# A mixture-of-experts layer on one core: in the experts' second matrix, high rows times high and low weights as one 512-column product in a bank of its own per row tile

## The chip, the cores and the metric

The kernel runs on one core of a Trainium2 chip. Time is device time in microseconds (us), from a run of the whole program. TensorE (PE) multiplies, ScalarE (ACT), VectorE (DVE) and GpSimd (POOL) work on rows and columns, SyncE (SP) issues most transfers. A core has eight PSUM banks of 512 float32 columns.

## What is computed

Three stages over 4096 rows of 256 columns: x + 0.5 FFN(norm x), then x + attention(norm x), then x + 0.5 FFN(norm x). The change touches the experts of both FFN stages:

```python
topk_w, topk_idx = jax.lax.top_k(scores, cap)       # 16 experts, 256 rows of each of 2 batches
x_tok = jnp.take_along_axis(hidden_states[:, None, :, :], topk_idx[..., None], axis=2)
g = jnp.einsum('becd,efd->becf', x_tok, Wg)
u = jnp.einsum('becd,efd->becf', x_tok, Wu)
h = jax.nn.gelu(g, approximate=False) * u           # 512 hidden columns
eo = jnp.einsum('becf,edf->becd', h, Wd) * topk_w[..., None]
flat = flat.at[flat_idx].add(eo.reshape(-1, d))
out = flat + shared                                 # the shared expert
```

## The kernel before

Each FFN stage goes through 24 items of 512 rows: items 0 to 7 are the shared expert on all rows, items 8 to 23 the 16 experts (J = 8, NI = 24). In the first FFN stage (`lead`) the last three items are mixed from two experts each. A float32 product is made of three on rounded parts: high x high, high x low, low x high (`product3`, lines 349 to 353). So columns, weights and hidden values each exist as a high part, made by ScalarE (a copy that rounds), and a low part, made by VectorE (the difference).

The engines work in steps s, each in an order written out by hand. In step s of the expert stretch:

- TensorE makes gate and up of item s - 1 in four pieces f, gu(s, 0) and gu(s, 1), then down of item d = s - 2 (`down`, line 905), then gu(s, 2) and gu(s, 3). A piece is 12 products of 512 columns into one bank of pG and one of pU. down is four row tiles q of 12 products of 256 columns, two tiles to a bank (pD). Before it writes a piece's pG bank, gelu of two pieces before must be done, and before the pU bank mul of two pieces before.
- ScalarE (lines 1156 to 1186): gelu(s, f) of each piece, high(s, f) of the hidden values, split(s, w) for the high part of the three weights of item s, join_planes(s) (two copies at L1069 and one at L1072), which joins the turned halves of item s's gathered columns (turned_planes, which the profile calls outing_turned_planes in the first and uting_turned_planes in the second stage), and part_planes(s + 1) (L1062), which parts the next item's rows into 16-bit planes.
- VectorE (lines 1518 to 1535): mul(s, f) = gelu x up into hf, low(s, f), split (low parts, L756), evacuate(s, 0), lower(s) (low part of the joined columns, L1308), evacuate(s, 1), gate_weights(s), split(s, 2), mul(s, 2) and so on. evacuate scales a half of down by the gate weight and 0.5 into the SBUF tile eo (L1333).
- SyncE: per expert load_weight for the three weights, each when VectorE has split the one before from the same buffer, and behind raw_d's load turn_planes (L773), a transposing transfer of the planes that part_planes made. Its landing releases join_planes one step on.
- POOL: four scatters of item s - 2's rows (L1571) after the evacuations, then four gathers of a later item's rows (L1547).

The last steps of the first FFN stage (s = 21 to 23) have an order of splits of their own on both engines (`last_steps`, line 1393, and lines 1166 to 1180).

## Time and profile before

| | |
|---|---|
| median of 3 runs | 1497.14 us (1496.7 to 1497.23) |
| profiled execution: its time | 1497.23 us |
| profiled execution: its span | 1495.5 us |
| busy in the span: PE | 1459.6 us (98%) |
| ACT | 1084.9 us (73%) |
| DVE | 891.5 us (60%) |
| POOL | 568.4 us (38%) |

The first FFN stage takes up the first third of the span, attention the middle, the second FFN stage the last third from some 1060 us on. Expert items run from about 190 to 455 and from about 1225 to 1490 us. A share over the whole span mixes these stages; what a change in the experts is worth is read from a step of theirs.

### The profile page before, as it was taken

To read this page: it belongs to the slowest core of one execution; us is meant where nothing else is said; L and a number is where in the kernel's file an instruction comes from. 1 tells how busy PE (TensorE), PEld (TensorE's weight loads), DVE (VectorE), ACT (ScalarE), POOL (GpSimd) and SP (SyncE) were. 2 spreads that over 40 slices of the span, in tenths; PEclk is the share of its full clock that TensorE was granted. 3 is DMA by queue.
4 is the path that set the end of the run, shared out by engine and by line. 5 is a ranking of instruction groups with operands and counts; after the bars stand their busy time and mean duration, and the time that the engine had idled before them with its cause. 6 is when DMAs were issued, how large, how long until landed. Compare 5 with 4: busy or idle time off the path is not lost. (4 is left out here: it accounts for less than half of the span.)

```text
span 1495.5 us, 26581 instructions
## 1 busy us (share of the span) xinstructions
PE 1459.6 (98%) x9857; PEld 1020.4 (68%) x9861; DVE 891.5 (60%) x1984; ACT 1084.9 (73%) x1391; POOL 568.4 (38%) x500
## 2 busy tenths in 40 slices
PE   5999999999999999999999999999999999999998
PEld 4788888888897763333343343333688888888887
DVE  7888777677657971222145152126788867776774
ACT  7322277777746889999999999999622247777772
POOL 5000357776546961112111121111300045666645
PEclk9999999999999999999999999999999999999999
DMA  9212287898846798505337162212511158878873
GB/s 306 78 57 71 87 222 181 187 201 198 192 71 187 248 282 181 87 1 87 51 83 136 33 130 45 43 61 68 159 50 67 57 162 176 214 181 194 194 164 43
DMA packets 180402, 195.74 MB, mean 131 GB/s; under 512 B 77296, under 2 KB 142320, under 8 KB 177520
## 3 DMA queue, kind: packets, MB, share of 16 engines
q1 hardware_dynamic: 152096, 146.30, 38.9%
q0 software_dynamic: 28176, 47.73, 15.1%
q8 instruction: 79, 1.29, 0.4%
q14 instruction: 51, 0.42, 0.1%
HBM read 123.73 MB, written 55.57 MB: 120 GB/s over the span
## 5 line engine op out<-in xcount | busy, mean ns | idle before, releaser
L2507 ACT ACTIVATE 6351_pr<-6351_pS 128x1024 f32<-128x1024 f32 x448 | 420.6, 1196 | 3.1 <-PE 6351_pS L2399 3.1
L2430 PE MATMUL 6351_pO<-6351_pr,6336_vres 128*32 128x512 f32 x1792 | 238.2, 605 | 0.0
L2399 PEld LDWEIGHTS 6351_pS<-sq_rows,sk_rows 50*128 50x128 f32 x896 | 77.7, 184 | 180.2 <-ACT 6351_pr L2507 133.6
L2399 PE MATMUL 6351_pS<-sq_rows,sk_rows 50*128 50x512 f32 x896 | 184.2, 469 | 2.3 <-issue 1.3
L2531 POOL TENSOR_SCALAR_AFFINE_SELECT 6351_pr<-6351_pr 128x512 f32<-128x512 f32 x32 | 20.5, 642 | 358.7 <-ACT 6351_pr L2507 358.7
L351 PE MATMUL 6362_pGU<-columns_ahead,weights_wts 128*128 128x512 f32 (+1 forms) x400 | 155.5, 389 | 0.2 <-DVE 6362_hf L1297 0.2
L352 PE MATMUL 6362_pGU<-columns_ahead,weights_wts 128*128 128x512 f32 (+1 forms) x400 | 152.6, 381 | 0.0
L353 PE MATMUL 6362_pGU<-columns_ahead,weights_wts 128*128 128x512 f32 (+1 forms) x400 | 152.4, 381 | 0.0
L351 PE MATMUL 93_pGU<-columns_ahead,weights_wts 128*128 128x512 f32 (+1 forms) x368 | 143.1, 389 | 1.7 <-issue 1.3
L1106 ACT ACTIVATE hidden_hT<-93_hf 128x512 fp32r<-128x512 f32 x96 | 60.6, 632 | 112.5 <-DVE 93_hf L1297 112.3
L352 PE MATMUL 93_pGU<-columns_ahead,weights_wts 128*128 128x512 f32 (+1 forms) x368 | 140.1, 381 | 0.0
L353 PE MATMUL 93_pGU<-columns_ahead,weights_wts 128*128 128x512 f32 (+1 forms) x368 | 139.9, 380 | 0.0
L1106 ACT ACTIVATE hidden_hT<-6362_hf 128x512 fp32r<-128x512 f32 (+1 forms) x100 | 61.4, 614 | 105.8 <-DVE 6362_hf L1297 105.8
L1571 POOL DMA_INDIRECT out<-eo,6362_idx x64 | 104.7, 1636 | 81.9 <-issue 44.9
L1571 POOL DMA_INDIRECT x_after_ffn<-eo,93_idx x60 | 101.9, 1699 | 77.0 <-DVE eo L1333 48.9
L2584 DVE TENSOR_TENSOR rows_acc<-6351_pO,rows_acc 128x512 f32<-128x512 f32 x30 | 20.8, 692 | 172.6 <-PE 6351_pO L353 172.5
L2541 DVE STREAM_TRANSPOSE 6351_tO<-6351_pO 128x512 f32<-128x512 f32 (+1 forms) x33 | 23.0, 699 | 156.4 <-PE 6351_pO L2430 155.3
L351 PE MATMUL 6362_pD<-weights_wts,hidden_hT 128*128 128x256 f32 x376 | 107.6, 286 | 0.0
L352 PE MATMUL 6362_pD<-weights_wts,hidden_hT 128*128 128x256 f32 x376 | 106.4, 283 | 0.0
L353 PE MATMUL 6362_pD<-weights_wts,hidden_hT 128*128 128x256 f32 x376 | 106.3, 283 | 0.0
L351 PE MATMUL 93_pD<-weights_wts,hidden_hT 128*128 128x256 f32 x352 | 100.8, 286 | 0.0
L352 PE MATMUL 93_pD<-weights_wts,hidden_hT 128*128 128x256 f32 x352 | 99.6, 283 | 0.0
(437 smaller groups left out, 3581.8 us busy)
## 6 DMA issues: line engine op xcount, KB each, us to landing
93_raw_g<-WgT SPq DMA_DIRECT2D x16, 512.0 KB
93_raw_u<-WuT SPq DMA_DIRECT2D x16, 512.0 KB, 3.9
93_raw_d<-WdT SPq DMA_DIRECT2D x16, 512.0 KB, 5.0
q_rows<-rows_halves SPq DMA_DIRECT2D x8, 1024.0 KB, 5.5
k_rows<-rows_halves SPq DMA_DIRECT2D x8, 1024.0 KB, 5.1
6362_raw_g<-WgT SPq DMA_DIRECT2D x16, 512.0 KB
6362_raw_u<-WuT SPq DMA_DIRECT2D x16, 512.0 KB, 3.7
6362_raw_d<-WdT SPq DMA_DIRECT2D x16, 512.0 KB, 4.6
```

The source lines that it names most:

```text
L351: pe.matmul(out, w_hi, x_hi, start=start, stop=False)
L352: pe.matmul(out, w_hi, x_lo, start=False, stop=False)
L353: return pe.matmul(out, w_lo, x_hi, start=False, stop=stop)
L1106: s_hh.done(a.activation(hT[0][:, i % 2, f, cut], hf[:, f % 2, cut], ACT.Copy))
L1571: sent = g.indirect_dma_start(out, bass.IndirectOffsetOnAxis(place_of(item, q), 0), eo[:, k, q, :], None, compute_op=ALU.add)
L2399: m = t_.matmul(to[:, e, :], key, query, start=True, stop=True)
L2430: m = t_.matmul(pO[e * 32:(e + 1) * 32, j % 2, off:off + wd], vres[:, (g // GB) * TPB + kt, at:at + 32], from_(e), start=n == first[j], st ...
L2507: s_exp.done(a.activation(to, pS[:, u % RING, :, :], ACT.Exp, scale=HD ** -0.5))
L2531: s_mask.done(g.affine_select(out=blk_, in_=blk_, compare_op=ALU.is_ge, fill=0.0, base=0, pattern=[[0, GH], [1, P]], channel_multiplier=-1))
L2541: s_copy.done(v.transpose(tO[:, part], pO[:, j % 2, part]))
L2584: s_free.done(v.tensor_tensor(two, from_.rearrange("p (t d) -> p t d", d=D), two, ALU.add))
```

## The change

For items 8 to 21 of either stage (`wide`), the high hidden rows are multiplied with the high and the low down weights side by side, as one product of 512 columns, into a bank of its own for each row tile: the two banks of pD, pX and pC (`wide_bank`). The low rows times the high weights stay a product of 256 columns, added to the first half of the bank. So the sum of a row tile stands in two halves. ScalarE takes the second half, scaled by the gate weight, into eo (`half_out`, L1102 of the changed kernel); VectorE adds the first half to it, scaled alike (L1374). The down weights lie so that high and low stand side by side for each chunk of rows. The factor 0.5 goes into the gate weights. The order of the splits at the end of the first stage comes from one function (`split_in`), and VectorE runs steps 21 to 23 in the common loop.

```diff
             def weight(k, w, h):
+                if w == 2:
+                    return down_pair(k)[:, :, h * D:(h + 1) * D]
                 return wts[k][:, 2 * w + h, :].rearrange("p (c f) -> p c f", c=FC if w == 2 else DC)
+
+            def down_pair(k):
+                return wts[k][:, 4:6, :].rearrange("p h f -> p (h f)").rearrange("p (c w) -> p c w", c=FC)
+
+            wide = lambda d: J <= d < NI - 2
+            wide_bank = lambda q: (pL(0), pX[:, :], pL(1), pC[:, :])[q]
...
+            def split_in(s, at):
+                if lead and s == NI - 3 and at >= 3:
+                    return [(s + 1, at - 3)]
+                if lead and s == NI - 2:
+                    return [(s, 2)] if at == 0 else [(s + 1, at - 1)] if at < 3 else []
+                if lead and s == NI - 1:
+                    return [(s, 2)] if at == 0 else []
+                return [(s, at)] if at < 3 else []
...
+                    if wide(d):
+                        last = c == FC - 1
+                        if c == 0:
+                            t_.matmul(to, hT[0][:, d % 2, c, rows_], down_pair(k)[:, c, :], start=True, stop=False)
+                        m = t_.matmul(to[:, 0:D], hT[1][:, d % 2, c, rows_], weight(k, 2, 0)[:, c, :], start=False, stop=False)
+                        if c > 0:
+                            m = t_.matmul(to, hT[0][:, d % 2, c, rows_], down_pair(k)[:, c, :], start=False, stop=last)
+                        return m
...
-                            m = rows_down(d, q, c, pD[:, q // 2, q % 2, :])
+                            m = rows_down(d, q, c, wide_bank(q) if wide(d) else pD[:, q // 2, q % 2, :])
...
+                def half_out(s, h):
+                    d = s - 2
+                    k = d % 2
+                    if not wide(d):
+                        return
+                    if h == 0:
+                        s_so[k].wait(a, J // 2)
+                        s_sc[k].wait(a, (d - J) // 2)
+                        s_wt.wait(a, d - J + 1)
+                    a.wait_ge(*s_D.at(2 * d + h + 1))
+                    for q in (2 * h, 2 * h + 1):
+                        m = a.activation(eo[:, k, q, :], wide_bank(q)[:, D:2 * D], ACT.Copy, scale=wt[:, k, q:q + 1])
+                    s_half.done(m)
...
-                        own_weights = s < NI - (2 if lead else 0)
                         gelu(s, 0)
-                        if own_weights:
-                            split(s, 0)
+                        splits(s, 0)
                         high(s, 0)
                         gelu(s, 1)
-                        if own_weights:
-                            split(s, 1)
+                        splits(s, 1)
                         high(s, 1)
-                        if lead and s == NI - 2:
-                            split(s, 2)
-                            split(s + 1, 0)
                         if s == BY_PE:
                             gathered(s)
                         else:
                             join_planes(s)
-                        if own_weights:
-                            split(s, 2)
+                        half_out(s, 0)
+                        splits(s, 2)
+                        half_out(s, 1)
+                        gelu(s, 2)
                         if lead and s == NI - 3:
-                            split(s + 1, 0)
-                            split(s + 1, 1)
-                        if lead and s == NI - 2:
-                            split(s + 1, 1)
-                            split(s + 1, 2)
-                        gelu(s, 2)
-                        if s < NI - 1:
+                            splits(s, 3)
+                        elif s < NI - 1:
                             part_planes(s + 1)
                         high(s, 2)
-                        hidden(s, 3)
+                        gelu(s, 3)
+                        splits(s, 4)
+                        if lead and s == NI - 3:
+                            part_planes(s + 1)
+                        high(s, 3)
                         continue
...
-                    v.wait_ge(*s_D.at(2 * d + h + 1))
+                    if wide(d):
+                        v.wait_ge(*s_half.at(2 * (d - J) + h + 1))
+                    else:
+                        v.wait_ge(*s_D.at(2 * d + h + 1))
                     for r in range(2):
                         q = 2 * h + r
-                        if d < J:
+                        if wide(d):
+                            m = v.scalar_tensor_tensor(eo[:, k, q, :], wide_bank(q)[:, 0:D], wt[:, k, q:q + 1], eo[:, k, q, :],
+                                                       ALU.mult, ALU.add)
+                        elif d < J:
                             m = v.scalar_tensor_tensor(eo[:, k, q, :], pD[:, h, r, :], 0.5, eo[:, k, q, :], ALU.mult, ALU.add)
                         else:
-                            m = v.tensor_scalar(eo[:, k, q, :], pD[:, h, r, :], wt[:, k, q:q + 1], 0.5, ALU.mult, ALU.mult)
+                            m = v.tensor_scalar(eo[:, k, q, :], pD[:, h, r, :], wt[:, k, q:q + 1], None, ALU.mult)
                     s_ev.done(m)
...
-                            m = v.tensor_copy(wt[:, item % 2, 2 * h:2 * h + 2].unsqueeze(1), by_weight[:, D + e:D + e + 1, 2 * h:2 * h + 2])
+                            m = v.tensor_scalar(wt[:, item % 2, 2 * h:2 * h + 2].unsqueeze(1), by_weight[:, D + e:D + e + 1, 2 * h:2 * h + 2], 0.5,
+                                                None, ALU.mult)
                     else:
-                        m = v.tensor_copy(wt[:, item % 2, :].unsqueeze(1), by_weight[:, D + item - J:D + item - J + 1, :])
+                        m = v.tensor_scalar(wt[:, item % 2, :].unsqueeze(1), by_weight[:, D + item - J:D + item - J + 1, :], 0.5, None, ALU.mult)
...
-                    if lead and s >= NI - 3:
+                    if lead and s >= NI:
                         last_steps(s)
                         continue
                     if s >= NI:
...
                             last_item(s)
                         continue
                     mul(s, 0)
-                    split(s, 0)
+                    splits(s, 0)
                     low(s, 0)
                     mul(s, 1)
-                    split(s, 1)
+                    splits(s, 1)
                     low(s, 1)
                     if s == BY_PE:
                         gathered(s)
...
                         lower(s)
                         evacuate(s, 1)
                     gate_weights(s)
-                    split(s, 2)
+                    splits(s, 2)
                     mul(s, 2)
+                    splits(s, 3)
                     low(s, 2)
                     mul(s, 3)
+                    splits(s, 4)
                     low(s, 3)
```

ScalarE in a step of the first stage's expert stretch, from the join of an item's columns to the first high part behind it. Before:

```order
L1069 ACTIVATE columns1_joined_102_103<-outing_turned_planes_116_117 128x1024 [waits 49_pe_U,49_planes_turned]
L1069 ACTIVATE columns1_joined_102_103<-outing_turned_planes_116_117 128x1024
L1072 ACTIVATE columns_ahead0_51<-columns1_joined_102_103 128x1024 [waits 49_act_joined]
L753 ACTIVATE weights0_wts_94_95<-93_raw_d 128x1024 [waits 49_pe_D,49_raw2]
L1098 ACTIVATE 93_gl<-93_pGU 128x512 [waits 49_dve_mul,49_pe_G]
L1062 ACTIVATE routing_planes_114_115<-93_xr 128x2048 [waits 49_planes_turned,49_gathered1]
L1106 ACTIVATE hidden_hT0_106_107<-93_hf 128x512 [waits 49_dve_mul]
```

Changed:

```order
L1110 ACTIVATE columns1_joined_102_103<-outing_turned_planes_116_117 128x1024 [waits 49_pe_U,49_planes_turned]
L1110 ACTIVATE columns1_joined_102_103<-outing_turned_planes_116_117 128x1024
L1113 ACTIVATE columns_ahead0_51<-columns1_joined_102_103 128x1024 [waits 49_act_joined]
L1102 ACTIVATE eo_58<-93_pD,93_wt 128x256 [waits 49_dve_wt,49_pe_D,49_scattered0,49_shared_out0]
L1102 ACTIVATE eo_58<-93_pX,93_wt 128x256
L772 ACTIVATE weights0_wts_94_95<-93_raw_d 128x4x256 [waits 49_pe_D,49_raw2]
L1102 ACTIVATE eo_58<-93_pD,93_wt 128x256 [waits 49_pe_D]
L1102 ACTIVATE eo_58<-93_pC,93_wt 128x256
L1139 ACTIVATE 93_gl<-93_pGU 128x512 [waits 49_dve_mul,49_pe_G]
L1089 ACTIVATE routing_planes_114_115<-93_xr 128x2048 [waits 49_planes_turned,49_gathered1]
L1147 ACTIVATE hidden_hT0_106_107<-93_hf 128x512 [waits 49_dve_mul]
```

Four operations that write eo (L1102) now stand between the join and gelu (L1098, now L1139): two ahead of the split of the down weights and two behind it.

VectorE, from the evacuation of the first half to mul(s, 2). Before:

```order
L1333 TENSOR_SCALAR eo_58<-93_pD,93_wt 128x256 [waits 49_dve_wt,49_pe_D,49_scattered1,49_shared_out1]
L1333 TENSOR_SCALAR eo_58<-93_pD,93_wt 128x256
L1308 TENSOR_TENSOR columns_ahead1_52<-columns1_joined_102_103,columns_ahead0_51 128x1024 [waits 49_act_xh]
L1333 TENSOR_SCALAR eo_58<-93_pD,93_wt 128x256 [waits 49_pe_D]
L1333 TENSOR_SCALAR eo_58<-93_pD,93_wt 128x256
L1368 COPY 93_wt<-93_xr 128x4 [waits 49_dve_ev]
L756 TENSOR_TENSOR weights1_wts_96_97<-93_raw_d,weights1_wts_96_97 128x1024 [waits 49_act_wh]
L1297 TENSOR_TENSOR 93_hf<-93_gl,93_pGU 128x512 [waits 49_act_hh,49_dve_hl,49_pe_U,49_act_gelu]
```

Changed:

```order
L1374 SCALAR_TENSOR_TENSOR eo_58<-93_pD,93_wt,eo_58 128x256 [waits 49_dve_wt,49_act_half,49_scattered1,49_shared_out1]
L1374 SCALAR_TENSOR_TENSOR eo_58<-93_pX,93_wt,eo_58 128x256
L1348 TENSOR_TENSOR columns_ahead1_52<-columns1_joined_102_103,columns_ahead0_51 128x1024 [waits 49_act_xh]
L1374 SCALAR_TENSOR_TENSOR eo_58<-93_pD,93_wt,eo_58 128x256 [waits 49_act_half]
L1374 SCALAR_TENSOR_TENSOR eo_58<-93_pC,93_wt,eo_58 128x256
L1414 TENSOR_SCALAR 93_wt<-93_xr 128x4 [waits 49_dve_ev]
L775 TENSOR_TENSOR weights1_wts_96_97<-93_raw_d,weights1_wts_96_97 128x4x256 [waits 49_act_wh]
L1337 TENSOR_TENSOR 93_hf<-93_gl,93_pGU 128x512 [waits 49_act_hh,49_dve_hl,49_pe_U,49_act_gelu]
```

The places are the same; the evacuations now wait for ScalarE's half (act_half) where they waited for TensorE (pe_D).

ScalarE in step 21 of the first stage, where weights of item 22 (columns0_wts) are split in the same step. Before:

```order
L1072 ACTIVATE columns_ahead0_51<-columns1_joined_102_103 128x1024 [waits 49_act_joined]
L753 ACTIVATE weights1_wts_96_97<-93_raw_d 128x1024 [waits 49_pe_D,49_raw2]
L753 ACTIVATE columns0_wts_98_99<-93_raw_g 128x1024 [waits 49_pe_U,49_raw0]
L753 ACTIVATE columns0_wts_98_99<-93_raw_u 128x1024 [waits 49_pe_U,49_raw1]
L1098 ACTIVATE 93_gl<-93_pGU 128x512 [waits 49_dve_mul,49_pe_G]
L1062 ACTIVATE routing_planes_114_115<-93_xr 128x2048 [waits 49_planes_turned,49_gathered0]
L1106 ACTIVATE hidden_hT0_106_107<-93_hf 128x512 [waits 49_dve_mul]
L1098 ACTIVATE 93_gl<-93_pGU 128x512 [waits 49_dve_mul,49_pe_G]
L1106 ACTIVATE hidden_hT0_106_107<-93_hf 128x512 [waits 49_dve_mul]
```

Changed:

```order
L1102 ACTIVATE eo_58<-93_pX,93_wt 128x256
L772 ACTIVATE weights1_wts_96_97<-93_raw_d 128x4x256 [waits 49_pe_D,49_raw2]
L1102 ACTIVATE eo_58<-93_pD,93_wt 128x256 [waits 49_pe_D]
L1102 ACTIVATE eo_58<-93_pC,93_wt 128x256
L1139 ACTIVATE 93_gl<-93_pGU 128x512 [waits 49_dve_mul,49_pe_G]
L772 ACTIVATE columns0_wts_98_99<-93_raw_g 128x1024 [waits 49_pe_U,49_raw0]
L1147 ACTIVATE hidden_hT0_106_107<-93_hf 128x512 [waits 49_dve_mul]
L1139 ACTIVATE 93_gl<-93_pGU 128x512 [waits 49_dve_mul,49_pe_G]
L772 ACTIVATE columns0_wts_98_99<-93_raw_u 128x1024 [waits 49_pe_U,49_raw1]
L1089 ACTIVATE routing_planes_114_115<-93_xr 128x2048 [waits 49_planes_turned,49_gathered0]
L1147 ACTIVATE hidden_hT0_106_107<-93_hf 128x512 [waits 49_dve_mul]
```

The two splits of item 22 (raw_g, raw_u), which stood ahead of gelu, stand behind the first and the second gelu, and the parting of the planes behind them.

On TensorE a row tile's 12 products of 256 columns (L351 to L353) are now 4 of 512 (L924, L927) and 4 of 256 (L925).

## Rows read from the trace of the kernel before

**Rows 1.** Stretch; busy PE, PEld, DVE, ACT, POOL (instructions); PEclk; DMA share; GB/s
```profile
1300.00:1400.00 100.00, 100.00 (x577) 88.61 (x577) 70.78 (x102) 75.39 (x92) 65.55 (x48) 1.00 0.81 191
```

**Rows 2.** TensorE timeline: start, duration (us), operation; down, then gate and up
```profile
202.58 0.28 PE L351 MATMUL 93_pD<-weights_wts,hidden_hT 128*128 128x256 f32 x1
...
208.33 0.40 PE L351 MATMUL 93_pGU<-columns_ahead,weights_wts 128*128 128x512 f32 x1
...
216.52 0.39 PE L351 MATMUL 93_pGU<-columns_ahead,weights_wts 128*128 128x512 f32 x1
```

**Rows 3.** ScalarE timeline: first item joined, and one item to the next
```profile
207.98 1.06 ACT L1072 ACTIVATE columns_ahead<-columns_joined 128x1024 fp32r<-128x1024 f32 x1
...
307.45 1.06 ACT L1072 ACTIVATE columns_ahead<-columns_joined 128x1024 fp32r<-128x1024 f32 x1
...
321.59 2.25 ACT L1069 ACTIVATE columns_joined<-outing_turned_planes 128x1024 uint16<-128x1024 uint16 x2 [0.78 <-DMA outing_turned_planes<-routing_planes]
323.93 1.06 ACT L1072 ACTIVATE columns_ahead<-columns_joined 128x1024 fp32r<-128x1024 f32 x1
```

**Rows 4.** VectorE timeline of the same item: lower, and mul(s, 2)
```profile
308.61 1.23 DVE L1308 TENSOR_TENSOR columns_ahead<-columns_joined,columns_ahead 128x1024 fp32r<-128x1024 f32 x1 [2.02 <-ACT columns_ahead L1072]
...
311.87 0.68 DVE L1297 TENSOR_TENSOR 93_hf<-93_gl,93_pGU 128x512 f32<-128x512 f32 x1
```

**Rows 5.** SyncE's queue: raw_d's load, and transposes of both stages
```profile
212.99 4.49 SPq L773 DMA_TRANSPOSE outing_turned_planes<-routing_planes  x1
...
229.27 4.24 SPq L773 DMA_TRANSPOSE outing_turned_planes<-routing_planes  x1
...
311.97 0.37 SPq L764 DMA_DIRECT2D 93_raw_d<-WdT  x1
312.44 4.83 SPq L773 DMA_TRANSPOSE outing_turned_planes<-routing_planes  x1
...
1247.64 5.19 SPq L773 DMA_TRANSPOSE uting_turned_planes<-routing_planes  x1
...
1265.97 3.59 SPq L773 DMA_TRANSPOSE uting_turned_planes<-routing_planes  x1
...
1297.00 4.20 SPq L773 DMA_TRANSPOSE uting_turned_planes<-routing_planes  x1
```

**Rows 6.** Single lines: durations in ns, least, median, most
```profile
L1331 DVE SCALAR_TENSOR_TENSOR eo<-93_pD,eo x32: 410/416/426, 60.4 to 185.4; 128x256 f32<-128x256 f32 x32
...
L1333 DVE TENSOR_SCALAR eo<-93_pD,93_wt x60: 473/476/484, 206.7 to 443.4; 128x256 f32<-128x256 f32 x60
...
L1850 ACT ACTIVATE 6336_vres<-6341_pV x32: 356/392/415, 476.1 to 546.7; 128x256 f32<-128x256 f32 x32
...
L1049 ACT ACTIVATE weights_xn<-hidden_xq,93_shift,93_rstd x24: 584/594/605, 13.1 to 31.1; 128x256 f32<-128x256 f32 x24
```

**Rows 7.** ScalarE timeline: the joins that those transposes were for
```profile
221.93 2.25 ACT L1069 ACTIVATE columns_joined<-outing_turned_planes 128x1024 uint16<-128x1024 uint16 x2 [1.08 <-DMA outing_turned_planes<-routing_planes]
...
237.42 2.24 ACT L1069 ACTIVATE columns_joined<-outing_turned_planes 128x1024 uint16<-128x1024 uint16 x2
...
1258.63 2.25 ACT L1069 ACTIVATE columns_joined<-uting_turned_planes 128x1024 uint16<-128x1024 uint16 x2 [3.10 <-DMA uting_turned_planes<-routing_planes]
...
1273.24 2.26 ACT L1069 ACTIVATE columns_joined<-uting_turned_planes 128x1024 uint16<-128x1024 uint16 x2
...
1305.41 2.24 ACT L1069 ACTIVATE columns_joined<-uting_turned_planes 128x1024 uint16<-128x1024 uint16 x2
```

**Rows 8.** Timelines of step 21: two splits for item 22, and TensorE
```profile
393.77 1.04 ACT L753 ACTIVATE columns_wts<-93_raw_u 128x1024 fp32r<-128x1024 f32 x1
...
397.24 1.22 DVE L756 TENSOR_TENSOR columns_wts<-93_raw_u,columns_wts 128x1024 fp32r<-128x1024 f32 x1
...
398.56 0.36 PE L351 MATMUL 93_pGU<-columns_ahead,weights_wts 128*128 128x256 f32 x1 [1.33 <-issue]
```

**Rows 9.** POOL timeline: the first scatter of an item
```profile
307.39 1.62 POOL L1571 DMA_INDIRECT x_after_ffn<-eo,93_idx  x1 [1.95 <-DVE eo L1333]
```

51 lines of the change are left out of this document (16 added, 35 removed).

## The prediction, made before the changed kernel was run

> **What bounds the kernel now.** I read the busy table by stretches first, then TensorE's timeline in one expert item, then the timelines of ScalarE, VectorE and SyncE's queue over the same item. TensorE is busy in all of a stretch of experts, at the upper level of its clock, 2.4 GHz (PEclk 1.00) [rows 1]. It starts one product after the other without a break: 48 products of 256 columns take 208.33 - 202.58 = 5.75 us, 0.1198 us each, and 36 of 512 columns take 216.52 - 208.33 = 8.19 us, 0.2275 us each [rows 2]. An item has 48 of either, so its period is 10.92 + 5.75 = 16.67 us, and TensorE sets it.
>
> What the reader is to see beside that: a second loop goes round once per item and is almost as long. Call L the start of ScalarE's copy at line 1072, which ends the joining of an item's gathered columns. From L = 307.45, VectorE makes the low columns (308.61, L + 1.16), evacuates, splits the down weights and starts mul(s, 2) at L + 4.42 [rows 3, 4]. The end of that split lets SyncE issue the next raw_d load (311.97, L + 4.52) and right behind it the transpose of the next item's planes (312.44, L + 4.99) [rows 5]. The join for which they are turned starts at 321.59, 9.15 us after the issue, with "<-DMA" as releaser, and the next L is 323.93, 2.34 us later [rows 3]. The sum is 4.99 + 9.15 + 2.34 = 16.48 us: 0.2 us under TensorE's 16.67. Where a transpose takes longer, ScalarE waits for it and makes it up later; TensorE sees nothing of that.
>
> **The change part by part. The products.** Per row tile, twelve products of 256 columns become four of 512 and four of 256; per item 48 x 0.1198 = 5.75 us becomes 16 x 0.2275 + 16 x 0.1198 = 5.56 us. That is 0.193 us less per item, all of it on TensorE's path; items 8 to 21 of both stages, 28 items, give **-5.4 us**. The columns are as many as before; what goes is the part of each product that is not columns, 0.1198 us against 256 / 2.4 GHz = 0.1067 us.
> By the Trainium skill ("TensorE: Matmul & The Clock Gate", section "Wait — 56ns, not 53.3ns?") that part is about 2.5 ns per product and not 13 ns, and 448 products fewer would give 1.1 us; the rows disagree, so the sum goes by the rows.
>
> **ScalarE's new operations.** Four operations of 128x256 per item, out of PSUM with a scale from SBUF. The nearest rows are a copy of that size out of PSUM without such an operand, 0.39 us, and one with a scale and a bias operand, 0.59 us [rows 6]; I take the middle, 0.49 us, and 0.39 us from start to start. ScalarE has room for 1.6 us per item. But the first pair stands behind the join, and VectorE's evacuation of the first half now waits for it, and lower(s) stands behind that evacuation on VectorE. Before, that evacuation was done before the join.
> The Trainium skill ("ScalarE: Activation LUTs", section "What ACT_TABLE_LOAD costs") makes it 186 + 0.833 x 256 + 93 = 492 ns, an estimate from that page; no row here has this form.
>
> **Where that lands.** ScalarE is free of the join at L + 0.96; the pair ends at L + 0.96 + 0.39 + 0.49 = L + 1.84; 0.10 us of handover (as between 308.51 and 308.61 [rows 3, 4]) and two evacuations of 0.416 us, 0.81 us together, put lower at L + 2.75 in place of L + 1.16: 1.59 us later. The second pair of evacuations gets 0.10 us shorter (0.416 for 0.476 us, twice [rows 6]), its ScalarE half ends at L + 3.6 and is no later than lower, so the split, mul(s, 2) and SyncE's two issues come **1.49 us later**: raw_d at L + 6.01, the transpose at L + 6.48, mul(s, 2) from L + 5.91 to L + 6.59. The planes themselves are parted by L + 5.9 and are not late. New loop: 6.48 + t + 2.34 us, where t is from issue to join; new period of TensorE: 16.67 - 0.19 = 16.48 us. **Break-even: t = 16.48 - 6.48 - 2.34 = 7.66 us.**
>
> t, where the transpose follows raw_d's load as closely as it now always will (0.47 us): first stage 8.94, at most 8.15, and 9.15 us, mean 8.75; second stage 10.99 for its first and at most 7.27 us [rows 5, 7]. With the load issued further ahead the second stage shows at most 8.41 us [rows 5, 7]; 12 more items there are alike. So for that stage I take 7.84, midway between 7.27 and 8.41.
>
> TensorE waits once mul(s, 2) ends after it wants the bank. It wants it 24 + 6 products of 512 columns after the end of down, 6.83 us; mul ends at L + 6.6. So L may come 0.2 us after down's end. At the first join L is 207.98 and down ends at 208.33, L = -0.35 [rows 2, 3]; I take the same for the second stage.
> First stage: the first turn gives -0.35 + 8.94 - 7.66 - 0.2 = 0.7 us of wait, ten more 8.75 - 7.66 = 1.09 us each: **+11.6 us**. Second stage: -0.35 + 10.99 - 7.66 - 0.2 = 2.8 us for the first, and 12 x 0.18 = 2.2 us: **+5.0 us**.
>
> **The order of the last splits of the first stage.** In step 21 TensorE already waits 1.33 us for a weight split of item 22 [rows 8]. Before, ScalarE made both of that item's high parts ahead of gelu(21, 2); now the second one stands behind gelu(21, 3), and its low part behind mul(21, 3) on VectorE. From the end of mul(21, 2), L + 6.6, at least a high part (1.04 us) and a low part (1.22 us [rows 8]) follow one after the other, L + 8.9, and TensorE wants them 5.46 us after down's end: with L 1.3 us after down's end (0.2 and one turn's 1.09) a wait of 4.7 us, where 1.1 stood in the sum and 1.3 in the kernel before, +2.3 us; a high hidden part and a gelu stand between, so I take **+3 us** (0 to +5). In step 22 splits are moved ahead, away from a wait of like size; I cost that at nothing.
>
> **POOL.** The scatters follow the evacuations and start some 3 us later; POOL had 1.95 us of idle time ahead of them [rows 9]. They all move with it, so its queue stays as long as it was; the gathers behind them land later before the parting of the planes. I take nothing for that; if the gathers came last, it would add to the same loop.
> SyncE's later loads (raw_g, raw_u) follow VectorE's splits and are not moved past anything. The scale of the gate weights by 0.5 is the same one operation.
>
> **Sum:** -5.4 + 11.6 + 5.0 + 3 = +14.2 us. The profiled run took 1497.23 us, 1495.5 of it span; the median is 1497.14 us, the same within 0.1. So 1497.1 + 14.2 = **1511.3 us**.
>
> **The rivals. Hidden after all** (the other side): the transposes take 7.66 us or less in the new phase, since they now share the DMA engines with the scatters in another order. For it: 7.27 and the bounds of 8.15 and 8.41, which are no more than bounds. Then the wait of step 21 is all that is left, with L early half of the 3 us: 1497.1 - 5.4 + 1.5 = 1493.2 us. It decides at t = 7.66 us.
> **The slow turn in both stages:** t = 8.75 us in the second stage too: 12 x 1.09 = 13.1 in place of 2.2: 1522.2 us. For it: the first stage, whose loads are the same; against it: 7.27.
> **The wide product is no cheaper than its two halves**, because a longer product may hold what the short ones showed as a fixed part: the gain of 5.4 us falls away, 1516.7 us. Against it: 0.2275 us is already what 512 columns take here.
> By the 2.5 ns of the Trainium skill's section named above it would be 1497.1 - 1.1 + 19.6 = 1515.6 us; the trace has 13 ns in its place.
> That the change doesn't do what it says is excluded by the order of the instructions: 32 products per item stand there in place of 48.
>
> **How the numbers follow.** Forecast 0.52, hidden 0.22, slow turn 0.18, no cheaper 0.08. About 0.2% is what a measurement of this kernel can tell from no change: 1494.1 to 1500.1 us. Faster: two thirds of the hidden case, 0.15. Same: the rest of it and the lowest of the forecast, where t is near 7.8 in both stages, 0.11. Slower: 0.74. The unknown of the ScalarE operation (0.1 us either way, twice before the issue) moves some 23 turns by 0.2 us, 5 us either way; t of the second stage between 7.27 and 8.41 moves it from 1509 to 1518; t of 9.15 in the first adds 4. The range 1492 to 1525 takes in most of the hidden case and half of the slow one.
>
> **What would show it.** Right: in most items the join starts with "<-DMA turned planes" as releaser, the transposes are issued 0.47 us behind raw_d's load, the period of an item in the first stage is near 17.6 us, and TensorE's first product of an item's second matrix has idle time ended by VectorE's hf. The wide products start 0.2275 us apart. Wrong: joins without waiting for DMA, an item period of 16.48 us, or idle time of TensorE that another engine ends; and if ScalarE's new operations last over 0.6 us or wait for more than TensorE, the chain was read wrongly.

## The result, and the profile of the changed kernel

The changed kernel took 1534.06 us (median of 5 runs, 1527.18 to 1536.29) beside 1497.14 us for the kernel before: a ratio of 1.024, 95% interval 1.0227 to 1.0253. It is slower, in the way that was forecast, by 37 us where 14 were forecast, and outside the range. The profiled execution took 1536.29 us, 1534.6 of it span, 39.1 more than the span before.

Read first the busy table by stretches (columns as in [rows 1]), here of the changed kernel: eleven items of the first stage, the steps after them, and twelve items of the second stage. The stretch 205 to 385 of the kernel before stands first.

```profile
205.00:385.00 180.00, 180.00 (x1035) 159.32 (x1034) 127.24 (x186) 136.51 (x162) 128.44 (x87) 1.00 0.85 192
...
205.00:409.00 204.00, 193.31 (x919) 158.17 (x918) 127.38 (x189) 156.46 (x216) 130.54 (x88) 1.00 0.78 177
409.00:421.00 12.00, 4.79 (x22) 4.28 (x21) 8.92 (x14) 8.06 (x12) 8.69 (x6) 0.72 0.60 116
1265.00:1490.00 225.00, 211.73 (x999) 172.28 (x998) 143.52 (x215) 171.91 (x237) 148.52 (x100) 1.00 0.80 175
```

TensorE now has idle time in the stretches where it had none, and 7.2 of 12 us at the end of the first stage. Who it waits for, and who waits for the transposes, stands in the waits of the changed kernel (total us, times, longest), first for 205 to 385 us, then for 1265 to 1490 us:

```profile
ACT columns_joined L1110 <- DMA outing_turned_planes<-routing_planes: 17.7, 9, 3.1
PE 93_pGU L351 <- DVE 93_hf L1337: 7.1, 9, 1.0
PEld 93_pGU L351 <- DVE columns_ahead L1348: 5.5, 5, 1.6
PE 93_pGU L351 <- ACT 93_gl L1139: 3.6, 4, 1.2
...
ACT columns_joined L1110 <- DMA uting_turned_planes<-routing_planes: 22.3, 12, 3.0
PE 6262_pGU L351 <- DVE 6262_hf L1337: 9.8, 11, 1.1
PE 6262_pGU L351 <- ACT 6262_gl L1139: 3.4, 5, 1.1
```

ScalarE waits for the transpose in nearly every item of both stages. TensorE waits at an up product of nearly every item for VectorE's hf, and in about half of the items also six products earlier, at the first gate product, where gelu and the low part of the item's columns end at almost the same time.

One item shows the loop. Timelines of ScalarE, VectorE, SyncE's queue and TensorE of the changed kernel (start, duration, operation, idle time and its releaser), each in order of time; they answer to [rows 3 to 5]:

```profile
279.56 1.06 ACT L1113 ACTIVATE columns_ahead<-columns_joined 128x1024 fp32r<-128x1024 f32 x1
280.53 0.46 ACT L1102 ACTIVATE eo<-93_pD,93_wt 128x256 f32<-128x256 f32 x1
280.88 0.46 ACT L1102 ACTIVATE eo<-93_pX,93_wt 128x256 f32<-128x256 f32 x1
...
296.50 2.26 ACT L1110 ACTIVATE columns_joined<-outing_turned_planes 128x1024 uint16<-128x1024 uint16 x2 [3.09 <-DMA outing_turned_planes<-routing_planes]
298.85 1.06 ACT L1113 ACTIVATE columns_ahead<-columns_joined 128x1024 fp32r<-128x1024 f32 x1
```
```profile
281.48 0.48 DVE L1374 SCALAR_TENSOR_TENSOR eo<-93_pD,93_wt,eo 128x256 f32<-128x256 f32 x1 [5.24 <-ACT eo L1102]
...
282.27 1.22 DVE L1348 TENSOR_TENSOR columns_ahead<-columns_joined,columns_ahead 128x1024 fp32r<-128x1024 f32 x1
...
284.39 1.22 DVE L775 TENSOR_TENSOR weights_wts<-93_raw_d,weights_wts 128x1024 fp32r<-128x1024 f32 x1
285.52 0.68 DVE L1337 TENSOR_TENSOR 93_hf<-93_gl,93_pGU 128x512 f32<-128x512 f32 x1
```
```profile
285.63 0.37 SPq L783 DMA_DIRECT2D 93_raw_d<-WdT  x1
286.12 5.96 SPq L792 DMA_TRANSPOSE outing_turned_planes<-routing_planes  x1
```
```profile
286.26 0.50 PE L351 MATMUL 93_pGU<-columns_ahead,weights_wts 128*128 128x512 f32 x1 [0.99 <-DVE 93_hf L1337]
...
290.51 0.39 PE L924 MATMUL 93_pD<-weights_wts,hidden_hT 128*128 128x512 f32 x1
290.74 0.40 PE L925 MATMUL 93_pD<-weights_wts,hidden_hT 128*128 128x256 f32 x2
290.97 0.40 PE L927 MATMUL 93_pD<-weights_wts,hidden_hT 128*128 128x512 f32 x1
291.20 0.28 PE L925 MATMUL 93_pD<-weights_wts,hidden_hT 128*128 128x256 f32 x1
...
291.92 0.39 PE L924 MATMUL 93_pX<-weights_wts,hidden_hT 128*128 128x512 f32 x1
```

With L = 279.56, lower starts at L + 2.71, mul(s, 2) at L + 5.96, raw_d is issued at L + 6.07 and the transpose at L + 6.56. The join follows 10.38 us after that, held by the transpose alone, and the next L 2.35 us later: 19.29 us for this item. A row tile's down takes 291.92 - 290.51 = 1.41 us.

The end of the first stage, in the changed kernel's timelines of VectorE and TensorE, with the granted clock of 3.6 us of it (stretch row, columns as above); it answers to [rows 8]:

```profile
416.15 1.22 DVE L775 TENSOR_TENSOR columns_wts<-93_raw_u,columns_wts 128x1024 fp32r<-128x1024 f32 x1
```
```profile
409.87 0.39 PE L353 MATMUL 93_pGU<-columns_ahead,weights_wts 128*128 128x512 f32 x1
417.47 0.55 PE L351 MATMUL 93_pGU<-columns_ahead,weights_wts 128*128 128x256 f32 x1 [7.21 <-DVE columns_wts L775]
417.82 0.41 PE L352 MATMUL 93_pGU<-columns_ahead,weights_wts 128*128 128x256 f32 x1
418.03 0.41 PE L353 MATMUL 93_pGU<-columns_ahead,weights_wts 128*128 128x256 f32 x1
```
```profile
417.40:421.00 3.60, 3.53 (x16) 3.56 (x17) 0.69 (x1) 1.50 (x4) 2.99 (x3) 0.50 0.96 171
```

TensorE stands still for 7.2 us at item 22's first product, and the 16 products behind it come 0.213 us apart, at a granted clock of 0.50 (1.2 GHz), where 256 columns otherwise take 0.12 us.

Idle time counts from the modelled end of a product. What a stall costs is the gap from start to start less 0.2267 us (0.12 for 256 columns). Counted so from all of TensorE's starts: 14.6 us in 30 gaps between 205 and 409; 7.6 us in the gap at 409.87 and the restart behind it, and 16 x 0.093 = 1.5 us of slower products; 18.6 us in 41 gaps between 1246 and 1490, and 2.9 us in 3 behind that, the last of them at 1503.21 with 15 slower products behind it, at a granted clock of 0.50 again: 15 x 0.093 = 1.4 us. The kernel before has 2.3 us at the corresponding places of step 21 and 22 and nothing in the items. With the products' own gain of 4.3 us (below), 14.6 + 9.1 - 2.3 + 21.5 + 1.4 - 4.3 = 40.0 us, where the span grew by 39.1; the way from the last down product of the first stage to the first of the second, with attention in it, took 1.3 us less (600.1 us, 601.4 before).

### The profile page after: what moved, and what is told of

It reads as the page before. It is cut to its first block and busy times, and to the rows that moved or that the text cites. A ratio compares the mean times of both kernels' runs of the same rounds, so it can differ in the third digit from the quotient of the medians.

```text
span 1534.6 us, 25849 instructions
## 1 busy us (share of the span) xinstructions
PE 1466.8 (96%) x9409; PEld 996.7 (65%) x9413; DVE 884.6 (58%) x1984; ACT 1120.7 (73%) x1503; POOL 581.4 (38%) x500
## 5 line engine op out<-in xcount | busy, mean ns | idle before, releaser
L2534 ACT ACTIVATE 6251_pr<-6251_pS 128x1024 f32<-128x1024 f32 x448 | 420.4, 1187 | 2.2 <-PE 6251_pS L2426 2.2
L2457 PE MATMUL 6251_pO<-6251_pr,6236_vres 128*32 128x512 f32 x1792 | 237.9, 605 | 0.0
L2426 PEld LDWEIGHTS 6251_pS<-sq_rows,sk_rows 50*128 50x128 f32 x896 | 77.4, 184 | 179.5 <-ACT 6251_pr L2534 133.2
L2426 PE MATMUL 6251_pS<-sq_rows,sk_rows 50*128 50x512 f32 x896 | 183.4, 467 | 2.6 <-issue 1.4
L351 PE MATMUL 6262_pGU<-columns_ahead,weights_wts 128*128 128x512 f32 (+1 forms) x400 | 158.3, 396 | 15.8 <-DVE 6262_hf L1337 11.6
L351 PE MATMUL 93_pGU<-columns_ahead,weights_wts 128*128 128x512 f32 (+1 forms) x368 | 145.1, 394 | 18.1 <-DVE 93_hf L1337 7.3
L353 PE MATMUL 6262_pGU<-columns_ahead,weights_wts 128*128 128x512 f32 (+1 forms) x400 | 153.3, 383 | 0.0
L352 PE MATMUL 6262_pGU<-columns_ahead,weights_wts 128*128 128x512 f32 (+1 forms) x400 | 153.2, 383 | 0.0
L1598 POOL DMA_INDIRECT out<-eo,6262_idx x64 | 108.6, 1698 | 95.0 <-issue 59.0
L353 PE MATMUL 93_pGU<-columns_ahead,weights_wts 128*128 128x512 f32 (+1 forms) x368 | 140.5, 382 | 0.0
L351 PEld LDWEIGHTS 6262_pGU<-columns_ahead,weights_wts 128*128 128x128 f32 x400 | 76.2, 191 | 37.8 <-DVE 6262_hf L1337 17.3
L2534 ACT ACTIVATE 6251_prs<-6251_pS 128x1024 f32<-128x1024 f32 x96 | 96.8, 1198 | 0.0
L351 PEld LDWEIGHTS 93_pGU<-columns_ahead,weights_wts 128*128 128x128 f32 x368 | 69.9, 190 | 36.8 <-DVE 93_hf L1337 11.9
L1574 POOL DMA_INDIRECT 93_xr<-token_table,93_idx x64 | 77.4, 1210 | 34.6 <-issue 19.2
L1574 POOL DMA_INDIRECT 6262_xr<-token_table,6262_idx x64 | 77.1, 1204 | 34.5 <-issue 19.5
```

Source lines behind the costliest of these rows:

```text
L351: pe.matmul(out, w_hi, x_hi, start=start, stop=False)
L352: pe.matmul(out, w_hi, x_lo, start=False, stop=False)
L353: return pe.matmul(out, w_lo, x_hi, start=False, stop=stop)
L1574: s_rows[k].part(g.indirect_dma_start(xr[:, k, q, :], None, self.table[:, :], bass.IndirectOffsetOnAxis(place_of(item, q), 0)), 16)
L1598: sent = g.indirect_dma_start(out, bass.IndirectOffsetOnAxis(place_of(item, q), 0), eo[:, k, q, :], None, compute_op=ALU.add)
L2426: m = t_.matmul(to[:, e, :], key, query, start=True, stop=True)
```

## The experiments

The theory (A): the transpose is issued later, behind a chain through ScalarE's new operations and VectorE, and so the loop over it is longer than TensorE's period. Its rivals: the new work itself on ScalarE and VectorE (B); the wide products (C); the gathers on POOL (D). Ratios are against the kernel before on the same chip. t is the time from the transpose's issue to its landing; its means are over 22 turns, turns 2 to 11 of the first stage and 2 to 13 of the second, from the updates of the semaphore that tells of the landing. The name of a run stands behind its heading.

**The transpose ahead of raw_d's load** (turn_first).
```diff
-                    for w in range(3):
-                        load_weight(e, w)
-                    turn_planes(J + e)
+                    load_weight(e, 0)
+                    load_weight(e, 1)
+                    turn_planes(J + e)
+                    load_weight(e, 2)
```


> The changed kernel with one thing moved on SyncE: the transpose of the next item's planes is issued ahead of the load of raw_d, and no longer behind it. Theory A (the loop over VectorE's split, raw_d's load, the transpose and the join sets the item's period): the transpose is issued once the planes are parted, about L + 4 us in place of L + 6.56, so the loop is 4 + t + 2.35 us: 15.6 us even with t = 9.2, under TensorE's 16.48. The two stages lose 10 x (18.2 - 16.5) + 12 x (18.1 - 16.5) = 36 us and the time is 1498 us, 1493 to 1503; the wait of 7.4 us in step 21 stays. With no load just ahead t itself should fall from 9.2 to 5 to 7 us. Rival B (ScalarE and VectorE have too much to do, or the gathers come too late): the period stays at 18 us and the time at 1528 to 1538 us. Rival C (the wide products are slow on TensorE): likewise unchanged, and TensorE is busy where it now waits.

Measured: 1505.9 us, ratio 1.0062 (1.0047 to 1.0077). In both stages TensorE has no gap in the items any more and ScalarE waits for no transpose; the items settle at 16.51 us. t fell from 9.1 to 5.5 us. All that with the wide products and ScalarE's operations in place, so rivals B and C fall. It is 8 us above the expectation, and what is missing lies behind the items: the loads of item 23 stand behind a transpose that waits for the late parting of step 21, and TensorE waits at two places (3.1 and 5.1 us by the gap from start to start less the product; two rows of its timeline in this kernel for the second). With 1.6 us of smaller gaps and slower products this is 9.8 us, where 7.4 stood in the expectation.

```profile
415.29 0.28 PE L353 MATMUL 93_pGU<-columns_ahead,columns_wts 128*128 128x256 f32 x1
420.47 0.35 PE L351 MATMUL 93_pGU<-columns_ahead,columns_wts 128*128 128x256 f32 x1 [4.90 <-DVE columns_wts L775]
```

Another 4.3 us lie behind that: from the last down product of the first stage to the first of the second it takes 605.8 us, and 601.4 in the kernel before. Why is not known.

**The wide products alone** (before_wide). In the kernel before; the second half of each bank is left out, that is hidden high times the low weights.
```diff
-                            m = rows_down(d, q, c, pD[:, q // 2, q % 2, :])
+                            m = rows_down(d, q, c, wide_bank(q) if wide(d) else pD[:, q // 2, q % 2, :])
...
-                            m = v.tensor_scalar(eo[:, k, q, :], pD[:, h, r, :], wt[:, k, q:q + 1], 0.5, ALU.mult, ALU.mult)
+                            m = v.tensor_scalar(eo[:, k, q, :], wide_bank(q)[:, 0:D] if wide(d) else pD[:, h, r, :], wt[:, k, q:q + 1], 0.5, ALU.mult, ALU.mult)
```


> The kernel before with the wide products alone: one bank per row tile, 16 products of 512 and 16 of 256 columns per item, but the second half of each bank is not added (that part of the down product is left out), so nothing is added on ScalarE, VectorE's evacuation waits for TensorE as before, and the order of the last splits is that of before. By the prediction's first term TensorE gains 28 x 0.193 = 5.4 us and nothing else changes: 1491.7 us, ratio 0.9964, 1490.5 to 1493. If a wide product is no cheaper than two halves: 1497.1 us, ratio 1.000. If the loop of the turns already limits at TensorE's new period of 16.48 us: between the two.

Measured: 1494.77 us, ratio 0.9988 (0.9979 to 0.9997), 1.8 us faster. TensorE has no gap in the items of either stage, so the wide products are not slower, and the loop still fits, though with little to spare: t is 8.8 us here, 5.0 + 8.8 + 2.34 = 16.1 us, and with no new work on it ScalarE waits for the transpose in most items of the second stage (a row of its waits, 1265 to 1460 us), where it waits for none in the kernel before.

```profile
ACT columns_joined L1085 <- DMA uting_turned_planes<-routing_planes: 8.3, 11, 2.1
```

Only a third of the expected gain is seen in the time, and 3.4 us in the span of its profile (1492.1 against 1495.5). Part of the shortfall is the item's period, 16.51 us in place of 16.48, against 16.66 before: 28 x 0.153 = 4.3 us, not 5.4. Where the rest goes was not found.

**ScalarE's first pair ahead of the join** (half0_early).
```diff
                         else:
+                            half_out(s, 0)
                             join_planes(s)
-                        half_out(s, 0)
```


> The changed kernel with ScalarE's first pair of new operations ahead of the join in place of behind it. They wait only for the first half of down, which ends before the join starts. Theory A: the pair's 0.71 us leaves the loop and VectorE's evacuation of that half is done before the join (up to another 0.9 us, so that lower starts 0.1 us behind the join): the issue of the transpose comes 0.7 to 1.6 us earlier, the period falls from 18.1 to 17.4 or, at best, to TensorE's 16.5, and 22 items give 16 to 36 us: 1500 to 1518 us. Rival B (the load of ScalarE and VectorE as such): no change, 1530 to 1538, since the same operations are done. If TensorE's first half came too late for ScalarE, the join itself would start late and the time would rise above 1540 us.

Measured: 1499.7 us, ratio 1.0019 (1.001 to 1.0029). The transpose is issued at L + 5.47, 1.1 us earlier than in the changed kernel, with raw_d's load still 0.47 us ahead; t is 8.2 us. One line moved, no work taken away, gives back 34 of the 37 us, just more than expected. Rival B falls a second time. Of the 2 us by which the loop got shorter, 1.1 are the earlier issue and 0.9 the shorter t; with t at 9.1 it would be 5.5 + 9.1 + 2.35 = 16.9 us, still over 16.51.

**Both pairs out of the loop** (halves_out).
```diff
                         else:
+                            half_out(s, 0)
                             join_planes(s)
-                        half_out(s, 0)
                         splits(s, 2)
-                        half_out(s, 1)
                         gelu(s, 2)
...
                             part_planes(s + 1)
+                        half_out(s, 1)
                         high(s, 2)
...
                         lower(s)
-                        evacuate(s, 1)
-                    gate_weights(s)
                     splits(s, 2)
                     mul(s, 2)
+                    if s > BY_PE:
+                        evacuate(s, 1)
+                    gate_weights(s)
```


> The changed kernel with both of ScalarE's pairs out of the way: the first ahead of the join, the second behind the parting of the planes; VectorE's evacuation of the second half and the gate weights stand behind mul(s, 2). Theory A: lower starts 0.1 us behind the join, the split of the down weights ends at L + 3.3, raw_d is issued at L + 3.4 and the transpose at L + 3.9 us; the loop is 3.9 + 9.2 + 2.35 = 15.5 us, under 16.48, and the time is that of the stages without waits, 1534 - 36 = 1498 us, 1494 to 1504. Rival B (the work as such): 1530 to 1538. Rival D (POOL): the second pair of scatters and the gathers behind it wait for the later evacuation, the parting of the planes becomes late, and the time lies between, 1505 to 1525, with ScalarE's parting ended by the gathers' DMA.

Measured: 1496.28 us, ratio 0.9998 (0.9989 to 1.0008). The transpose is issued at L + 4.3 in most items; every period of the second stage is 16.51 us but for the last (16.82; 16.97 in the kernel before), and TensorE has no gap in the items of either stage. Rival D can be seen and costs nothing: ScalarE's waits of this kernel, 205 to 385 us, have the parting wait for the gathers five times, but the transpose still lands 1.6 us or more before its join.

```profile
ACT routing_planes L1089 <- DMA 93_xr<-token_table,93_idx: 2.9, 5, 1.1
```

What is left of the loss here is the gap of step 21, 4.1 us and 1.3 us of slower products behind it.

**The same, with the products parted again** (halves_narrow; the diff is against halves_out).
```diff
                         if c > 0:
-                            m = t_.matmul(to, hT[0][:, d % 2, c, rows_], down_pair(k)[:, c, :], start=False, stop=last)
+                            t_.matmul(to[:, 0:D], hi, weight(k, 2, 0)[:, c, :], start=False, stop=False)
+                            m = t_.matmul(to[:, D:2 * D], hi, weight(k, 2, 1)[:, c, :], start=False, stop=c == FC - 1)
```


> The kernel halves_out with each row tile's 512-column products parted again into 256 columns, save the first one of a tile (3 of 4 parted, 12 per item; same banks, same halves, same evacuation). In halves_out the period is TensorE's, 16.50 us, against 16.66 before. If the wide product is what gains, 12 x (2 x 0.1198 - 0.2275) = 0.145 us per item return: period 16.65, 28 x 0.145 = 4.1 us, 1500.4 us. If the gain comes from elsewhere (banks, fewer waits): 1496.3 us as halves_out.

Measured: 1499.14 us, the median of eleven runs from 1496.4 to 1503.85 us (a twelfth took 5795 us and is left out), ratio 1.002 (1.0009 to 1.0031), 2.9 us above halves_out, whose interval it just leaves. The period says it better: it is 16.60 us, so 0.09 us per item for 12 parted products, 0.008 us for each, where [rows 2] gave 0.012, and 28 x 0.09 = 2.6 us in all. The wide product gains, and less than the sum had it.

**The order of the splits of step 21** (best; against halves_out; their old places in that step go).
```diff
+                        if lead and s == NI - 3:
+                            splits(s, 3)
+                            splits(s, 4)
                         gelu(s, 2)
...
                     splits(s, 2)
+                    splits(s, 3)
+                    splits(s, 4)
                     mul(s, 2)
```


> The changed kernel with both of ScalarE's pairs out of the loop, as in halves_out, and with the splits of step 21 in another order: ScalarE makes both of item 22's high parts before gelu(21, 2) and VectorE both low parts before mul(21, 2). In halves_out TensorE stood still 4.1 us at item 22's first product and ran at 1.2 GHz for 1.3 us' worth of products behind it. Here the low part should end at L + 5.8 us where TensorE wants it at L + 4.7: about 1.1 us of wait and no slower products, 4 us less than halves_out's 1496.3: 1492 us, ratio to before 0.997, 1490.5 to 1494. Rival: item 22's raw_u has not landed by then, or the later mul(21, 2) only moves the wait to the next product: 1496 us as halves_out.

Measured: 1493.79 us, ratio 0.998 (0.9971 to 0.9988). The wait at item 22 fell to 1.0 us as expected; the rest came out at item 23, with a gap of 2.1 us, since its loads stand behind the late transpose.

**And the parting of step 21 where it was** (best_parted; against best).
```diff
                         gelu(s, 2)
-                        if lead and s == NI - 3:
-                            pass
-                        elif s < NI - 1:
+                        if s < NI - 1:
                             part_planes(s + 1)
...
                         gelu(s, 3)
-                        if lead and s == NI - 3:
-                            part_planes(s + 1)
                         high(s, 3)
```


> The kernel best with one thing put back as in the kernel before: in step 21 ScalarE parts the next item's planes behind gelu(21, 2), not behind gelu(21, 3). In best the parting of that step starts at 398.00 us, the transpose is issued at 399.93 and item 23's raw_g is loaded only behind it, at 402.26; ScalarE waits 4.7 us for that load, item 22's join comes 4.2 us after down's end and TensorE stands still 2.1 us. Here the transpose is issued some 3 us earlier, the join comes at least 2 us earlier and the wait of 2.1 us goes: 2 us less than best, 1491.8 us, ratio 0.9967, 1490.5 to 1493. Rival: raw_g's load is limited by something else and nothing changes: 1493.8 us.

Measured: 1491.79 us, ratio 0.9964 (0.995 to 0.9977): 5.2 us faster than the kernel before, and the best of all kernels here. Two rows of TensorE's timeline and two stretches (205 to 385, and behind the restart) of this kernel:

```profile
395.32 0.39 PE L353 MATMUL 93_pGU<-columns_ahead,weights_wts 128*128 128x512 f32 x1
396.55 0.36 PE L351 MATMUL 93_pGU<-columns_ahead,weights_wts 128*128 128x256 f32 x1 [0.84 <-issue]
```
```profile
205.00:385.00 180.00, 180.00 (x873) 151.59 (x872) 124.91 (x186) 149.66 (x208) 123.92 (x84) 1.00 0.87 191
...
396.60:400.00 3.40, 3.40 (x29) 3.40 (x30) 2.75 (x7) 2.00 (x6) 0.74 (x1) 1.00 1.19 285
```

TensorE is busy throughout, as in [rows 1], and it keeps its upper clock behind the short wait.

**The late transpose without the new work** (before_late). The kernel before, with VectorE's order turned; products and ScalarE are untouched.
```diff
-                    low(s, 1)
                     if s == BY_PE:
+                        low(s, 1)
                         gathered(s)
                     else:
+                        lower(s)
                         evacuate(s, 0)
-                        lower(s)
                         evacuate(s, 1)
+                        low(s, 1)
                     gate_weights(s)
```


> The kernel before, with its narrow products and nothing on ScalarE, but with VectorE's order turned: lower(s) first, then both evacuations and low(s, 1), then the gate weights and the split of the down weights. That moves the end of the split, raw_d's load and the transpose about 1.4 us later, to L + 5.95 and L + 6.4, and the first scatter some 2 us later, with no more work on any engine. Theory A (the lateness of the transpose is the loss): with t = 9.2 us the loop is 6.4 + 9.2 + 2.34 = 17.95 us, 1.3 us over TensorE's 16.66, and 22 items give +28 us: 1525 us, 1512 to 1530; with t of 8 us +2 us: 1499. Rival B (the new operations and products are the loss): 1497 us.

Measured: 1502.86 us, ratio 1.0037 (1.0022 to 1.0051). The transpose is issued at L + 6.27, as late as wanted, and ScalarE waits for it nine times (the row is from its waits, 205 to 385 us):

```profile
ACT columns_joined L1069 <- DMA outing_turned_planes<-routing_planes: 9.1, 9, 2.2
```

But t was 8.1 us and not 9.2: by the same loop, 6.27 + 8.1 + 2.34 = 16.7 us, just over TensorE's 16.66. The direction is as theory A has it, the size hangs on t, and the gaps in the items come to only 2 us; step 21 adds to it, with a gap of 3.8 us in place of 1.5, and so does the end of the second stage, with gaps of 1.5 and 0.3 us and slower products behind them. (The profiled run took 1507.52 us.) So lateness alone did not yet reproduce the loss, and why t was 9.1 in the changed kernel was open.

**What lengthens the transpose.** First with 7 of 8 rows of the wide items' scatters left out, then also with the transpose ahead of the load, then with whole scatters moved a little later.
```diff
-                        sent = g.indirect_dma_start(out, bass.IndirectOffsetOnAxis(place_of(item, q), 0), eo[:, k, q, :],
+                        n_ = 16 if J <= item < NI - 2 else P
+                        sent = g.indirect_dma_start(out, bass.IndirectOffsetOnAxis(place_of(item, q)[0:n_], 0), eo[0:n_, k, q, :],
```


> The changed kernel with 7 of 8 rows of the wide items' scatters left out (16 rows in place of 128 for each of the four scatters of an item, so most of these experts' sum is not added), all else as it is. It tells why the transpose takes 9.2 us from issue to join in the changed kernel. If the scatters that now fall beside it (at -0.8, +1.3 and +3.2 us from its issue) lengthen it: t falls to 8 us or less, the period to 17 us or less and the time to 1500 to 1515 us. If raw_d's load 0.47 us ahead of it is all there is to it: t stays at 8.8 to 9.3 us and the time at 1524 to 1536 us.

> The changed kernel with 7 of 8 rows of the wide items' scatters left out and with the transpose issued ahead of raw_d's load. With the scatters left out alone t was 6.5 us, with the transpose moved ahead alone 5.5 us, with neither 9.2. If each lengthens the transpose on its own, t is 4 to 5 us here; if either alone was enough for a bare transpose, t stays at 5.3 to 5.6 us. The time is no lower than turn_first's by more than 3 us, 1500 to 1507 us, since the loop no longer sets the period in either.

```diff
+                    if item < NI - 2:
+                        g.wait_ge(*s_xl.at(lowered(item + 3)))
                     for q in range(4):
```


> The changed kernel with the wide items' first scatter made to wait for lower(s) too, so that all four scatters, and the gathers behind them, start about 1.1 us later against the transpose: at -1.8, +0.3, +2.4, +4.3 us from its issue in place of -2.9, -0.8, +1.3, +3.2. It asks why the transpose took 9.2 us in the changed kernel and 8.1 in before_late, with raw_d's load 0.47 us ahead of it in both. If the phase of the scatters makes the difference: t falls to about 8 us, the period from 18.1 to 17.0, and the time is 1510 us, 1503 to 1518, unless the later gathers hold the parting of the planes (then nearer to 1525). If the phase is nothing: t 9.2, 1530 to 1540 us.

Measured: 1504.31 us (thin_scatter), 1507.66 us (thin_turn_first) and 1521.3 us (scatter_later), two runs each. The runs beside each other, with the typical starts of the item's four scatters against the issue of the transpose:

| kernel | raw_d's load before the issue | scatters at (us) | mean t |
|---|---|---|---|
| before | 0.47 to 1.4 us | -4.9, -3.0, -1.1, 0.8 | 7.7 |
| before_wide | 0.47 to 1.2 | -4.8, -2.9, -0.9, 1.1 | 8.8 |
| changed | 0.47 | -2.9, -0.8, 1.3, 3.2 | 9.1 |
| half0_early | 0.47 | -5.9, -4.0, -1.0, 1.2 | 8.2 |
| scatter_later | 0.47 | -1.8, 0.1, 2.0, 3.9 | 8.2 |
| before_late | 0.47 | -2.3, 0.1, 2.0, 3.9 | 8.1 |
| halves_out | 0.76 to 2.0 | -4.1, -2.2, 2.4, 4.3 | 6.5 |
| thin_scatter | 0.47 | as changed, 1/8 of the rows | 6.6 |
| turn_first | 1.4 to 2.7 behind | -2.5, -0.4, 1.7, 3.7 | 5.5 |
| thin_turn_first | 1.4 to 1.7 behind | as turn_first, 1/8 of the rows | 4.6 |

The three other runs built on halves_out have 6.0 to 6.4 us. The load and the scatters each lengthen the transpose on their own: the load by 2 us (4.6 to 6.6), the scatters by 0.9 (4.6 to 5.5), both together by 4.5, more than the sum. How near the load is counts even where the scatters stay in their places: in the kernel before, the seven turns with the load 0.47 to 0.50 us ahead have a mean t of 8.8 us and the fourteen with 1.3 to 1.4 us one of 7.1, and in before_wide the fourteen with 0.47 to 0.53 us have 8.9. With scatter_later t fell by 0.9 us as expected, for the same load and the same bytes, and the time by 13 us: where the scatters lie against the transpose counts too, or the gathers behind them, which moved along; the runs do not part the two. The time did not come down to 1510 us and missed its range: TensorE still has 6.6 us of gaps between 205 and 400, 8.1 between 1255 and 1475, and 6.3 in step 21. In thin_scatter and thin_turn_first the items have next to no gaps (none, and 0.5 us in all). What stands above 1497 us is outside them: gaps and slower products at the end of the first stage (4.6 and 6.5 us, 2.5 in the kernel before), 3 to 4 us more between the stages, and 6.7 us more behind the last down product of the program; the last two are not explained. Thin_scatter's time is in its expected range, thin_turn_first's 0.7 us above it. That single transposes of one kernel differ by 2.5 us (7.9 to 10.4 in the changed one) is not explained.

## Why the prediction was right and wrong

- **The mechanism** was right in each of its signs. Joins start with "<-DMA", raw_d is 0.47 us ahead of the transpose, TensorE waits at the up product for hf. That moving one line of ScalarE's gives 34 us back, and both pairs all of it in the items, shows it. The wait at the first gate product was not foreseen.
- **The chain from L** was right: lower L + 2.71 (2.75 forecast), mul(s, 2) L + 5.96 (5.91), the transpose L + 6.54 to 6.56 (6.48). ScalarE's operation took 0.46 to 0.48 us and 0.36 from start to start (0.49 and 0.39). VectorE's evacuation took 0.48 us and not 0.416, so the second pair got no shorter; the two misses nearly cancel. By the Trainium skill ("ScalarE: Activation LUTs", section "What ACT_TABLE_LOAD costs") it would be 492 ns, an estimate from that page; the medians of 462 to 481 ns are 2 to 6% below that.
- **t of the second stage is the step that failed.** The sum took 7.84 us there, midway between a join with the load 0.47 us ahead (at most 7.27) and one with the load further ahead (at most 8.41). It measured 9.1, as in the first stage. 12 x (9.1 - 7.84) = 15 us, out of the 23 us by which the forecast was low: 21.5 us of gaps in place of 5.0. The mistake was to take t in part from a phase that the change itself removes. The prediction says that the load will always be 0.47 us ahead; in the second stage of the kernel before, it is 1.3 to 1.4 us ahead in eleven turns of fourteen, as in these two rows of SyncE's queue, and those landed after 6.9 us on the mean:

```profile
1312.27 0.37 SPq L764 DMA_DIRECT2D 6362_raw_d<-WdT  x1
1313.66 2.81 SPq L773 DMA_TRANSPOSE uting_turned_planes<-routing_planes  x1
```

  The five turns of [rows 5, 7] with the load 0.47 us ahead have, over both stages, a mean of 8.9 us; that the two stages differ rested on a single turn (7.27). The change also moves the scatters on to the transpose, and the runs show that their place counts; but in before_wide, with the scatters where they were, t is 8.8 us, so the nearer load gives most of the rise. The rival "slow turn in both stages" (0.18) was what happened; its own t of 8.75 was still low.
- **t of the first stage**: 8.75 taken, 9.1 measured; 14.6 us of gaps in place of 11.6.
- **The end of the first stage**: forecast +3 us, and found 9.1 - 2.3 = 6.8 us, part of it the last turn's. Two terms were missed: the wait follows an item whose L lay 2.5 us after down's end and not 1.3, and TensorE's slower products behind it, 1.5 us.
- **TensorE's gain**: 5.4 us forecast. The period is 16.51 us, not 16.48, from 16.66 and not 16.67: 4.3 us. A row tile takes 1.41 us where 4 x 0.2275 + 4 x 0.1198 = 1.39 was counted. In the time, the gain showed as 1.8 us in before_wide and 2.9 us between halves_out and halves_narrow. By the 2.5 ns per product of the Trainium skill ("TensorE: Matmul & The Clock Gate", section "Wait — 56ns, not 53.3ns?") the 336 products that halves_narrow adds would cost 0.8 us, an estimate from that page; the trace disagrees, 8 ns each by the period.
- **POOL** at nothing was right as far as the gathers go: in the changed kernel ScalarE's parting waits for none of them between 205 and 385 us. What its scatters do to the transposes was not in the sum.
- **The range** ended at 1525 us since it took t between 7.27 and 8.41 in the second stage alone. With both stages at the longest of the first stage in the rows, 9.15 us, the same sum gives 10 x 0.4 + 12 x 1.31 = 19.7 us more, 1531 us. The rows had that number.

## What to carry to other kernels

A loop through a DMA that is 1% shorter than the bound engine's period has no room: before adding work to an engine that is off the bound, follow what the next instructions of its queue release. Place such work off the chain that leads to the issue on which the loop hangs, here one pair ahead of the join and one behind the parting; the two reordered pairs took away the loss of 37 us, and with the splits of one step put in another order the kernel became 5 us faster than the one before. And a transfer's duration belongs to its phase: if the change moves it among other transfers, take it from the turns that already lie so, and from them alone.

## What the runs showed of the hardware

- A transpose of the planes from SBUF to SBUF took 4.6 us from issue to landing with little beside it (thin_turn_first), 6.6 us with a 512 KB load issued 0.47 us ahead on the same queue (thin_scatter), 5.5 us with scatters beside it (turn_first), and 8.1 to 9.1 us with both, by their phase. In the kernel before it took 8.8 us with the load 0.47 to 0.50 us ahead and 7.1 us with 1.3 to 1.4 us.
- Behind 7.2 us of standing still TensorE ran 16 products at a granted clock of 0.50 (1.2 GHz) before it was back at 1.00; behind 0.84 us in best_parted it stayed at 1.00. The length of the wait alone did not decide it: behind 2.9 us at item 22 (398 us in both runs) the clock stayed at 1.00 in turn_first and fell to 0.50 in thin_scatter, and in the changed kernel it fell to 0.50 behind a wait of 1.65 us (at 1503.21).
